# Attention runs of a four-layer hybrid stack: accumulator begun behind the first products, other order of transfers, root first on ScalarE, one table for exp and ln

## The chip, the cores and the metric

One core of a Trainium2 chip runs the whole program. The metric is the device time of one execution in microseconds; the median of three runs is the time of the kernel.

## What is computed

The reference is a stack of four layers on `x` of shape (2, 512, 256), fp32. Each layer takes a layer norm of `x`, and adds the output of a sequence part and of a feed-forward part, both computed from the normed `xn`:

```python
xn = _layernorm(x)
x = x + attention0(xn) + mixture0(xn)      # 16 heads of 128, rotary, 32 experts
xn = _layernorm(x)
x = x + state_space(xn) + spline_mlp(xn)
xn = _layernorm(x)
x = x + linear_recurrence(xn) + table_mlp(xn)
xn = _layernorm(x)
x = x + attention3(xn) + mixture3(xn)      # 16 heads of 128, biases on q, k, v and out, 8 experts
```

Attention is causal. In layer 3 the output has a bias row, `out = attn @ w_o + b_o`. The linear recurrence of layer 2 needs, once, a few numbers per state that come from exp, ln, sin, cos and a root of its 32 parameters (`mag`, `theta`, `gamma`).

## The kernel before

The batch has two sequences of 512 positions. A sequence is held as four tiles of 128 rows (`x_of`), its norm turned into `xnT` (256 features on two times 128 partitions by 512 positions), and split into a high and a low part for products of nearly full precision: `exact_product` (line 201) issues three matmuls, high by high, and the two cross terms. `acc` is an accumulator of two PSUM banks that gathers what is added to `x`: the attention heads, then the experts.

The kernel is written engine by engine, with semaphores. A `Stage` holds one function per engine, and `run(m, *stages)` (line 162) makes one block: on each engine the stages' functions run in the order in which the stages are given. A block ends on all engines before the next begins. So what sets the order of work here is the order written in each engine's function, and the order of the stages in a `run`.

There are four attention runs: layer 0 for sequence 0 (from the program's start), layer 0 for sequence 1 (from 393 us), layer 3 for sequence 0 (from 1227 us) and layer 3 for sequence 1 (from 1525 us). In each, SyncE (SP) first issues the transfers of the weights of heads 0 and 1 (`load`, `load_values`, in `first_sync`), then small tables: in layer 0 the two rotary tables, in layer 3 the biases of q, k and v, a row of ones, and the output bias `bo` twice, side by side, into `bo_row`. All the small ones count on one semaphore, `rope_loaded`. ScalarE (ACT) copies each weight's high part, GpSimd (POOL) subtracts it for the low part (`head_low`, line 812). TensorE (PE) then begins `acc`: in layer 0 by `clear_acc` (line 2190, two bf16 matmuls of zeros), in layer 3 by two fp32 matmuls of the row of ones and `bo_row` (line 1003), 512 columns each. It goes on with head 0's q and k (`project`, 12 matmuls of 512 columns), half of the values (`project_v`, 12 matmuls of 256 columns), waits until this half has been stored (`v_ready`, and in layer 3 also `v_low`), projects the other half, and comes to the scores of head 0. From there `step` runs head by head.

The vector engine (DVE) in its function of the attention first does `ahead.begin_vector` (line 1115; in the runs in which the mixture follows in the same block, that is all but the first): a memset of `logits`, a wait for the router's transfers, and in layer 3 two small multiplies that scale `router` (line 1572). Only then come the rotation or the low parts of q, k and v, and the softmax of each head.

The first run has more stages in its block:

```python
run(m, constants, first, Norm(m, 0, 0, (0, 1)).stage(), decay, heads)
```

`first` holds the copies of the first weights, `Norm(...).stage()` the layer norm (DVE takes statistics, ACT the square root in `root`, line 586, DVE the reciprocal and `xn`, PE transposes, ACT stores, DVE the low parts), and `decay` the numbers of the recurrence: `scalar` on ACT (lines 246 to 260) and `vector` on DVE (lines 267 to 291) hand results to each other. On ACT the order is that of the stages: five weight copies, then the root, then the four stores of `xnT`, then decay, then the attention. A function whose table is not the active one is preceded by a load of its table, ACT_TABLE_LOAD. Beside the first run, POOL also builds the rows of the spline weights (`SplineRows.make`, lines 373 and 379), with the low parts of the heads' weights at fixed points in between.

## Time and profile before

| what | value |
|---|---|
| median of three runs | 1826.14 us (1825.59 to 1828.66) |
| the profiled execution, its own time | 1823.52 us |
| its span | 1821.7 us |
| granted TensorE clock, mean | 0.955 |
| PE busy | 1576.4 us (87%) |
| DVE busy | 1235.7 us (68%) |
| ACT busy | 936.3 us (51%) |
| POOL busy | 691.5 us (38%) |

The times are medians over whole executions; the profile is one execution, with each instruction's start and duration on the engine that ran it. The busy shares are averages over stages with different limits. A timeline row may merge several like instructions: then its second number is the length of the stretch, and "x4" says how many there were. A number in brackets is how long the engine had been idle before, and the name behind the arrow is what released it. For a matmul, the distance between two starts is what it occupies the engine; its own duration contains the drain of the pipeline.

### The profile page before, as it was taken

The page shows a single profiled execution, that of the slowest core. Times are in us where ns is not written, and L with a number is a line of the kernel's source. Part 1 is how long each engine was busy: PE and PEld are TensorE (multiplying, and loading weights), DVE is VectorE, ACT ScalarE, POOL GpSimd, SP SyncE. Part 2 cuts the span into 40 slices and gives each one's busy share as a digit, 9 for nine tenths or more (in the row PEclk, how much of TensorE's full clock was granted, in tenths as well). Part 3 has the DMA queues.
Part 4 walks back from the last instruction along what each step waited for, and adds up shares of the span by engine and source line. Part 5 has one row for each costly group of instructions (what it writes and reads, how often), then busy time and mean ns, then how long its engine had stood idle before and what let it go on. Part 6 is the DMA issues. An engine that isn't in the chain of part 4 may idle for free. (4 is left out here: it accounts for less than half of the span.)

```text
span 1821.7 us, 26108 instructions
## 1 busy us (share of the span) xinstructions
PE 1576.4 (87%) x8448; PEld 1221.7 (67%) x8448; DVE 1235.7 (68%) x2586; ACT 936.3 (51%) x1976; POOL 691.5 (38%) x624
## 2 busy tenths in 40 slices
PE   5989868979998988867876887888999897999889
PEld 3767658967776888334533444666888685788777
DVE  5888747757777778599968996444666534666643
ACT  5555445756665565554435543224665443666543
POOL 4999833324222222075714765102221232222232
PEclk9999989989999999989998999998999898999999
DMA  3212122111112220100010000001112111111111
GB/s 111 82 64 66 35 95 81 59 51 33 46 46 86 75 76 14 49 1 1 1 49 1 0 1 6 7 10 51 41 46 75 35 69 56 33 46 46 54 68 46
DMA packets 29708, 82.47 MB, mean 45 GB/s; under 512 B 6054, under 2 KB 10924, under 8 KB 27324
## 3 DMA queue, kind: packets, MB, share of 16 engines
q1 hardware_dynamic: 28444, 75.10, 12.6%
q0 software_dynamic: 1184, 6.37, 1.0%
q8 instruction: 42, 0.69, 0.2%
q14 instruction: 38, 0.31, 0.1%
HBM read 80.41 MB, written 1.05 MB: 45 GB/s over the span
## 5 line engine op out<-in xcount | busy, mean ns | idle before, releaser
L812 POOL TENSOR_TENSOR head_low<-head,head_high 128x512 fp32r<-128x512 f32 x64 | 81.8, 1279 | 474.3 <-ACT head_high L802 473.6
L2168 POOL TENSOR_TENSOR rings<-xp,Bs 128x512 f32<-128x512 f32 x128 | 193.7, 1515 | 163.1 <-DVE state L2107 82.9
L1708 POOL TENSOR_TENSOR experts_low<-experts,experts_high 128x1536 fp32r<-128x1536 f32 (+1 forms) x64 | 144.4, 2260 | 280.6 <-ACT experts_high L1654 161.1
L1161 ACT ACTIVATE probs<-banks,neg_max 128x512 f32<-128x512 f32 (+3 forms) x256 | 131.7, 527 | 150.2 <-DVE neg_max L1072 150.2
L1956 PE MATMUL banks<-rings,ident 128*128 128x512 f32 x256 | 140.3, 648 | 66.1 <-DVE rings L2136 66.1
L2107 DVE TENSOR_TENSOR_SCAN state<-banks,rings 128x512 f32<-128x512 f32 x128 | 155.4, 1215 | 0.0
L2042 ACT ACTIVATE banks<-delta,A 128x512 f32<-128x512 f32 x128 | 88.4, 692 | 119.2 <-DVE state L2107 108.3
L201 PE MATMUL banks<-experts_high,xnT_high 128*128 128x384 f32 (+1 forms) x384 | 139.9, 364 | 8.0 <-POOL experts_low L1708 8.0
L1405 DVE SCALAR_TENSOR_TENSOR hidden<-banks,weight,act_out 128x96 f32<-128x96 f32 (+1 forms) x192 | 62.7, 368 | 115.7 <-ACT act_out L1373 115.2
L201 PE MATMUL banks<-experts_low,xnT_high 128*128 128x384 f32 (+1 forms) x384 | 137.9, 359 | 0.0
L201 PE MATMUL banks<-experts_high,xnT_low 128*128 128x384 f32 (+1 forms) x384 | 137.6, 358 | 0.0
L1373 ACT ACTIVATE act_out<-banks 128x256 f32<-128x256 f32 (+2 forms) x112 | 47.5, 424 | 172.9 <-PE banks L201 172.7
L1956 PEld LDWEIGHTS banks<-rings,ident 128*128 128x128 f32 x256 | 47.0, 199 | 114.1 <-DVE rings L2136 85.7
L915 PE MATMUL banks<-ident,probs 128*128 128x128 f32 x640 | 87.7, 287 | 40.9 <-DVE probs L1080 40.9
L1169 ACT ACTIVATE probsT<-banks 128x384 f32<-128x384 f32 (+3 forms) x192 | 88.1, 527 | 66.0 <-PE banks L915 65.2
L1070 DVE TENSOR_REDUCE row_max<-banks 128x1 f32<-128x512 f32 (+3 forms) x256 | 110.6, 483 | 10.2 <-PE banks L906 9.9
L201 PE MATMUL banks<-xnT_high,head_high 128*128 128x512 f32 x256 | 109.8, 429 | 6.3 <-POOL head_low L812 6.3
L915 PEld LDWEIGHTS banks<-ident,probs 128*128 128x128 f32 x640 | 73.1, 146 | 50.4 <-DVE probs L1080 50.3
L1043 DVE TENSOR_TENSOR rot<-banks,rope_sin 32x512 f32<-32x512 f32 x128 | 87.2, 681 | 28.3 <-PE banks L201 25.0
L201 PE MATMUL banks<-xnT_low,head_high 128*128 128x512 f32 x256 | 103.8, 405 | 0.0
L1080 DVE TENSOR_SCALAR probs<-probs,row_inv 128x512 f32<-128x512 f32 (+3 forms) x256 | 102.0, 461 | 2.3
L201 PE MATMUL banks<-xnT_high,head_low 128*128 128x512 f32 x256 | 102.8, 402 | 0.0
(284 smaller groups left out, 4752.3 us busy)
## 6 DMA issues: line engine op xcount, KB each, us to landing
head<-in_heads SPq DMA_DIRECT2D x64, 384.0 KB, 3.1
experts<-in_experts SPq DMA_DIRECT2D x16, 1152.0 KB, 5.2
experts<-in_experts SPq DMA_DIRECT2D x16, 768.0 KB, 4.3
values<-in_values SPq DMA_DIRECT2D x32, 256.0 KB, 3.2
coef<-in_spline_coef POOLq DMA_DIRECT2D x8, 768.0 KB, 4.7
idx<-in_lut_idx SPq DMA_DIRECT2D x16, 134.0 KB, 2.1
Cs<-in_w_in SPq DMA_DIRECT2D x2, 1024.0 KB, 4.9
x<-in_x SPq DMA_DIRECT2D x2, 512.0 KB, 4.5
```

What stands on the lines that cost most here:

```text
L201: last = nc.tensor.matmul(out, left[a], right[b], start=start and n == 0, stop=stop and n == 2, **kw)
L915: last = nc.tensor.transpose(out[:, (i - k) * P:(i - k + 1) * P], prob_tile(i)[:, k * P:(k + 1) * P], m.ident[:])
L1043: chain.link(nc.vector.tensor_tensor(rot[to:to + 32, which], qk_psum[of:of + 32, which], rope_sin[of:of + 32], ALU.mult))
L1070: chain.link(nc.vector.reduce_max(row_max[:, i:i + 1], score_tile(i), AXIS.X))
L1080: last = nc.vector.tensor_scalar(prob_tile(i), prob_tile(i), row_inv[:, i:i + 1], None, ALU.mult)
L1161: last = nc.scalar.activation(prob_tile(i), score_tile(i), ACT.Exp, bias=neg_max[:, i:i + 1], scale=QK_SCALE, accum_out=row_sum[:, i:i + 1])
L1169: nc.scalar.activation(probsT[:, at:at + cols], m.banks[:, k, 0:cols], ACT.Copy)\
L1708: nc.gpsimd.tensor_tensor(parts[gpar][1][:, columns], raw[gpar][:, columns], parts[gpar][0][:, columns].bitcast(FP32), ALU.subtract)\
L1956: nc.tensor.matmul(y_psum(c), m.ident[:], product[:, step % PRODUCTS], start=n == 0, stop=n == NS - 1)\
L2042: nc.scalar.activation(decay_psum(step), delta[:, c], ACT.Exp, scale=A[:, c, n:n + 1])\
L2107: nc.vector.tensor_tensor_scan(state[:, step % 3], decay_psum(step), inflow[:, step % INFLOWS], 0.0, ALU.mult, ALU.add).then_inc(scanned.s ...
L2168: nc.gpsimd.tensor_tensor(inflow[:, step % INFLOWS], du[:, c], Bs[:, n], ALU.mult)\
```

## The change

It has six parts.

1. In all four attention runs, PE begins `acc` not before `project(0, 0)` but after `project_v(0, 0)`, ahead of the wait for `v_ready`.
2. In layer 3, `bo_row` is one row of 256 instead of two; the matmul reads it twice by a stride of zero, and one transfer is gone.
3. In layer 3, the transfer of the q, k and v biases is issued second, right behind head 0's weights, and has a semaphore of its own, `bias_loaded`, for which ACT and DVE wait. PE waits for `rope_loaded` at 32 (ones and `bo`) ahead of the bias matmuls.
4. DVE does `ahead.begin_vector` after head 0's low parts (layer 3) or rotation (layer 0) and the values' low parts, right ahead of the loop over the heads.
5. In the first run, the five weight copies on ACT are no longer a stage of their own ahead of the norm's; they run inside it between the root and the stores.
6. In `decay`, ACT first loads one table set that has both exp and ln.

```diff
         act.wait_ge(loaded.sem, loaded.at(16 * len(constants)))
 
         chain = Chain(act, act_chain)
+        nc.scalar.preload_act_table_set("natural_log_exp_and_others")
         chain.all(nc.scalar.activation(lru[:, 0:1], lru_in[:, 0:1], ACT.Abs))
...
-    def stage(self):
+    def stage(self, beside_root):
...
         def scalar(act):
             self.root(act)
+            beside_root(act)
             self.store(act, 0)
             self.store(act, 1)
...
-    rope_loaded = m.sig("rope_loaded")
+    rope_loaded, bias_loaded = m.sig("rope_loaded"), m.sig("bias_loaded")
...
-        bo_row, one_row = sb("bo_row", [1, 2, D]), sb("one_row", [1, P])
+        bo_row, one_row = sb("bo_row", [1, D]), sb("one_row", [1, P])
...
     def first_sync(sp):
-        for i in range(2):
-            load(sp, i, i)
-            load_values(sp, i, i)
+        load(sp, 0, 0)
+        if not rotary:
+            sp.dma_start(biases[:], m.dram["biases3"]).then_inc(bias_loaded.sem, 16)
+        load_values(sp, 0, 0)
+        load(sp, 1, 1)
+        load_values(sp, 1, 1)
         if rotary:
             sp.dma_start(rope_cos[:], m.dram["rope_cos"]).then_inc(rope_loaded.sem, 16)
             sp.dma_start(rope_sin[:], m.dram["rope_sin"]).then_inc(rope_loaded.sem, 16)
         else:
-            sp.dma_start(biases[:], m.dram["biases3"]).then_inc(rope_loaded.sem, 16)
             sp.dma_start(one_row[:], m.dram["ones"]).then_inc(rope_loaded.sem, 16)
-            for half in range(2):
-                sp.dma_start(bo_row[:, half, :], m.dram["bo"]).then_inc(rope_loaded.sem, 16)
+            sp.dma_start(bo_row[:], m.dram["bo"]).then_inc(rope_loaded.sem, 16)
...
+        project(0, 0)
+        pe.wait_ge(values_split.sem, values_split.at(1))
+        project_v(0, 0)
+
         if rotary:
             clear_acc(m, pe)
         else:
-            pe.wait_ge(rope_loaded.sem, rope_loaded.at(64))
+            pe.wait_ge(rope_loaded.sem, rope_loaded.at(32))
             for h in range(2):
-                nc.tensor.matmul(m.acc[:, h, :], one_row[:], bo_row[:].rearrange("o a d -> o (a d)"), start=True,
-                                 stop=False, skip_group_check=True)
-        project(0, 0)
-        pe.wait_ge(values_split.sem, values_split.at(1))
-        project_v(0, 0)
+                nc.tensor.matmul(m.acc[:, h, :], one_row[:], bo_row[:].unsqueeze(1).broadcast_to([1, 2, D]),
+                                 start=True, stop=False, skip_group_check=True)
...
-        if ahead:
-            ahead.begin_vector(dve)
-        dve.wait_ge(rope_loaded.sem, rope_loaded.at(32 if rotary else 64))
         if rotary:
+            dve.wait_ge(rope_loaded.sem, rope_loaded.at(32))
             chain = Chain(dve, dve_chain)
             turn(0, 0, chain)
             turn_rest(0, chain)
         else:
+            dve.wait_ge(bias_loaded.sem, bias_loaded.at(16))
             low_of_qk(0, 0)
             low_of_qk(0, 1).then_inc(qk_ready.sem, 1)
         spread_v(0, 0, 0)
         spread_v(1, 1, 0)
+        if ahead:
+            ahead.begin_vector(dve)
...
-                run(m, constants, first, Norm(m, 0, 0, (0, 1)).stage(), decay, heads)
+                split_weights, first.scalar = first.scalar, None
+                run(m, constants, first, Norm(m, 0, 0, (0, 1)).stage(split_weights), decay, heads)
```

How the instructions stand on ACT at the program's start (`rs` is the root, `head_high` and `values_high` are the weight copies, `xnT` and `xnT_high` the stores). Before:

```order
L802 ACT_TABLE_LOAD
L802 ACTIVATE head_high_3<-head_3 128x512
L807 ACTIVATE values_high_3<-values_3 128x512
L845 ACTIVATE head_high_3<-head_3 128x256
L802 ACTIVATE head_high_3<-head_3 128x512
L807 ACTIVATE values_high_3<-values_3 128x512
L586 ACT_TABLE_LOAD
L586 ACTIVATE rs<-rs 128x4
L620 ACTIVATE xnT<-banks 128x512
L622 ACTIVATE xnT_high<-banks 128x512
L620 ACTIVATE xnT<-banks 128x512
L622 ACTIVATE xnT_high<-banks 128x512
```

After the change:

```order
L587 ACT_TABLE_LOAD
L587 ACTIVATE rs<-rs 128x4
L805 ACTIVATE head_high_3<-head_3 128x512
L810 ACTIVATE values_high_3<-values_3 128x512
L849 ACTIVATE head_high_3<-head_3 128x256
L805 ACTIVATE head_high_3<-head_3 128x512
L810 ACTIVATE values_high_3<-values_3 128x512
L621 ACTIVATE xnT<-banks 128x512
L623 ACTIVATE xnT_high<-banks 128x512
L621 ACTIVATE xnT<-banks 128x512
L623 ACTIVATE xnT_high<-banks 128x512
```

The root and the load of its table went to the front, and the separate table load of the copies is gone.

On ACT right behind, in decay (`lru`). Before:

```order
L247 ACT_TABLE_LOAD
L247 ACTIVATE lru<-lru 64x1
L248 ACTIVATE lru<-lru_in 64x1
L249 ACT_TABLE_LOAD
L249 ACTIVATE lru<-lru 64x1
L252 ACTIVATE lru<-lru 64x1
L253 ACT_TABLE_LOAD
L253 ACTIVATE lru<-lru 64x1
L254 ACTIVATE lru<-lru 64x1
L257 ACT_TABLE_LOAD
L257 ACTIVATE lru<-lru 64x1
L258 ACTIVATE lru<-lru 64x1
```

After the change:

```order
L246 ACT_TABLE_LOAD
L247 ACTIVATE lru<-lru_in 64x1
L248 ACTIVATE lru<-lru 64x1
L249 ACTIVATE lru<-lru_in 64x1
L250 ACTIVATE lru<-lru 64x1
L253 ACTIVATE lru<-lru 64x1
L254 ACTIVATE lru<-lru 64x1
L255 ACTIVATE lru<-lru 64x1
L258 ACT_TABLE_LOAD
L258 ACTIVATE lru<-lru 64x1
L259 ACTIVATE lru<-lru 64x1
L261 ACT_TABLE_LOAD
```

Before, these rows have four table loads, and a fifth (L260) follows ahead of the last root; after, they have three, of which the first stands ahead of all of decay.

On PE at the start of the third attention run, before:

```order
L163 UNCONDITIONAL_BRANCH
L170 UNCONDITIONAL_BRANCH
L1003 MATMUL acc<-bo_row,one_row 128x512 x2
L201 MATMUL banks<-xnT_high,head_high_12 128x512
L201 MATMUL banks<-xnT_low,head_high_12 128x512
L201 MATMUL banks<-xnT_high,head_low_12 128x512
```

After the change, at the same place, and then around the end of the first half of the values:

```order
L163 UNCONDITIONAL_BRANCH
L170 UNCONDITIONAL_BRANCH
L201 MATMUL banks<-xnT_high,head_high_12 128x512
L201 MATMUL banks<-xnT_low,head_high_12 128x512
L201 MATMUL banks<-xnT_high,head_low_12 128x512
```

```order
L201 MATMUL banks<-values_high_12,xnT_high 128x256
L201 MATMUL banks<-values_low_12,xnT_high 128x256
L201 MATMUL banks<-values_high_12,xnT_low 128x256
L1011 MATMUL acc<-bo_row,one_row 128x512 x2
L201 MATMUL banks<-values_high_12,xnT_high 128x256
L201 MATMUL banks<-values_low_12,xnT_high 128x256
L201 MATMUL banks<-values_high_12,xnT_low 128x256
```

The two matmuls of `bo_row` went from the front to behind the 24 first products; the fourth run shows the same, and the first two the same with the clearing of `acc`.

On DVE at the start of the third attention run, before and after the change:

```order
L176 UNCONDITIONAL_BRANCH
L1567 MEMSET logits 128x4x6
L1572 TENSOR_SCALAR router<-router,router_scale 128x8 x2
L1028 SCALAR_TENSOR_TENSOR qkT_low<-banks,biases,qkT 128x512 x2
L1062 TENSOR_TENSOR v_low_12<-banks,v_12 128x512 x2
L1126 UNCONDITIONAL_BRANCH
L1126 ISA
L1070 TENSOR_REDUCE row_max<-banks 128x1
```

```order
L176 UNCONDITIONAL_BRANCH
L1033 SCALAR_TENSOR_TENSOR qkT_low<-banks,biases,qkT 128x512 x2
L1067 TENSOR_TENSOR v_low_12<-banks,v_12 128x512 x2
L1573 MEMSET logits 128x4x6
L1578 TENSOR_SCALAR router<-router,router_scale 128x8 x2
L1132 UNCONDITIONAL_BRANCH
L1132 ISA
L1075 TENSOR_REDUCE row_max<-banks 128x1
```

The memset and the two multiplies of the router now stand between the low parts of the values and the loop of the heads, which begins with `row_max` of head 0's scores.

## Rows read from the trace of the kernel before

**Rows 1.** the chain that ended last, start of the fourth attention run: start us, us, what

```profile
1528.23 3.64 DMA bo_row<-in_bo
1531.91 3.78 PE acc L1003 x4
```

**Rows 2.** timeline, ScalarE (ACT), first attention run: start us, us, engine line, what, [idle before <- releaser]

```profile
13.06 0.63 ACT L807 ACTIVATE values_high<-values 128x512 fp32r<-128x512 f32 x1 [0.79 <-DMA values<-in_values]
13.71 1.28 ACT L586 ACT_TABLE_LOAD   x1
...
18.30 0.60 ACT L620 ACTIVATE xnT<-banks 128x512 f32<-128x512 f32 x1 [3.09 <-PE banks L613]
...
19.75 0.62 ACT L622 ACTIVATE xnT_high<-banks 128x512 fp32r<-128x512 f32 x1
...
28.90 1.02 ACT L1144 ACTIVATE qkT<-banks 64x1024 f32<-64x1024 f32 x1
```

**Rows 3.** timeline, VectorE (DVE), first attention run

```profile
6.62 0.17 DVE L570 TENSOR_SCALAR rs<-mv 128x4 f32<-128x4 f32 x1
...
22.21 0.15 DVE L270 TENSOR_SCALAR turns<-lru 64x1 int32<-64x1 f32 x1 [1.07 <-ACT lru L248]
...
23.51 0.24 DVE L534 TENSOR_TENSOR lru<-lru 64x1 f32<-64x1 f32 x1
...
24.60 1.52 DVE L534 TENSOR_TENSOR lru<-lru 64x1 f32<-64x1 f32 x1
...
27.95 2.82 DVE L1043 TENSOR_TENSOR rot<-banks,rope_sin 32x512 f32<-32x512 f32 x4
```

**Rows 4.** timeline, TensorE (PE), first attention run

```profile
21.24 1.00 PE L2190 MATMUL acc<-mask_bf,ident_bf 1*128 1x512 bf16 x2 [2.12 <-DVE xnT_low L629]
...
33.33 1.12 PE L902 MATMUL banks<-qkT 128*128 128x512 f32 x2 [1.03 <-DVE qkT L1054]
```

**Rows 5.** timeline, GpSimd (POOL), first attention run

```profile
21.32 1.39 POOL L373 TENSOR_SCALAR spline_rows<-coef,points 128x256 f32<-128x256 f32 x3 [4.11 <-DMA coef<-in_spline_coef]
...
43.48 1.27 POOL L812 TENSOR_TENSOR head_low<-head,head_high 128x512 fp32r<-128x512 f32 x1 [12.70 <-ACT head_high L802]
```

**Rows 6.** waits of POOL, 47 to 205 us: in total us, times, longest us

```profile
POOL head_low L818 <- ACT head_high L1185: 8.0, 7, 1.2
```

**Rows 7.** timeline, PE, second attention run

```profile
400.25 0.80 PE L201 MATMUL banks<-xnT_high,head_high 128*128 128x512 f32 x1 [6.30 <-POOL head_low L812]
...
407.94 0.38 PE L201 MATMUL banks<-values_high,xnT_high 128*128 128x256 f32 x1 [0.69 <-ACT v L1155]
```

**Rows 8.** timeline, PE, third attention run

```profile
1233.71 3.77 PE L1003 MATMUL acc<-bo_row,one_row 1*128 1x512 f32 x4 [8.07 <-DMA bo_row<-in_bo]
1237.42 0.79 PE L201 MATMUL banks<-xnT_high,head_high 128*128 128x512 f32 x1
...
1245.50 0.35 PE L201 MATMUL banks<-values_high,xnT_high 128*128 128x256 f32 x1 [1.50 <-DVE v_low L1062]
```

**Rows 9.** timeline, PE, fourth attention run

```profile
1535.62 0.80 PE L201 MATMUL banks<-xnT_high,head_high 128*128 128x512 f32 x1
...
1543.11 0.36 PE L201 MATMUL banks<-values_high,xnT_high 128*128 128x256 f32 x1 [1.50 <-DVE v_low L1062]
```

**Rows 10.** timeline, POOL, third attention run

```profile
1230.98 1.27 POOL L812 TENSOR_TENSOR head_low<-head,head_high 128x512 fp32r<-128x512 f32 x1 [46.53 <-ACT head_high L802]
```

**Rows 11.** timeline, POOL, fourth attention run

```profile
1529.36 1.26 POOL L812 TENSOR_TENSOR head_low<-head,head_high 128x512 fp32r<-128x512 f32 x1 [20.98 <-ACT head_high L802]
```

**Rows 12.** timeline, DVE, third attention run

```profile
1234.21 2.42 DVE L1572 TENSOR_SCALAR router<-router,router_scale 128x8 f32<-128x8 f32 x2 [6.81 <-DMA per_expert<-in_per_expert]
...
1247.82 0.69 DVE L1062 TENSOR_TENSOR v_low<-banks,v 128x512 fp32r<-128x512 f32 x1 [2.47 <-ACT v L1155]
1248.43 1.70 DVE L1070 TENSOR_REDUCE row_max<-banks 128x1 f32<-128x512 f32 x4
```

**Rows 13.** windows: stretch, us, busy of PE PEld DVE ACT POOL (instructions), PEclk, DMA, GB/s

```profile
1237.00:1242.00 5.00, 5.00 (x12) 3.62 (x12) 0.75 (x1) 0.69 (x1) 0.00 (x0) 0.50 0.11 42
```

More of the change, by code:

```diff
@@ L1203, in scalar @@
         if not rotary:
-            act.wait_ge(rope_loaded.sem, rope_loaded.at(64))
+            act.wait_ge(bias_loaded.sem, bias_loaded.at(16))
         spread_rest(0)
@@ L1248, in close @@
             s.close(PAIRS)
+        rope_loaded.close(32)
         if rotary:
             qk_rest_ready.close(HEADS)
-            rope_loaded.close(32)
         else:
-            rope_loaded.close(64)
+            bias_loaded.close(16)
             qk_high.close(2 * HEADS)
```

## The prediction

> **What bounds the kernel now.** The page says that PE is busy for 87% of the span, but the change touches only the first microseconds of the four attention runs, so the shares say little; what counts is the last wait in each of these stretches. I read the chain that ended last first, then the timeline of each engine at each start, then POOL's waits.
>
> The chain shows the start of the fourth run: the transfer of `bo_row` (3.64 us), then the matmuls that put it into the accumulator (3.78 us) [rows 1]. PE has the first products behind them. In the third run it is the same: PE is idle for 8.07 us until `bo_row` lands, and the first product starts at 1237.42 [rows 8], although its weights were ready when POOL's `head_low` ended, at 1230.98 + 1.27 = 1232.25 [rows 10]. In the second run nothing is ahead of the products but `head_low` [rows 7].
>
> In the first run the root comes late: DVE had its input at 6.79, while ACT, with the copies ahead of it, was done with the last copy at 13.69 and only then loaded the root's table [rows 2, 3]. The stores of `xnT` (18.30 to 20.37) wait for PE, thus for the root. Then ACT and DVE play decay back and forth: DVE's part starts at 22.21, it is free for the rotation at 27.95, ACT for `qkT` at 28.90 [rows 2, 3], and the first scores start at 33.33, released by DVE [rows 4]. The reader should see that both queues are in order: heads wait behind decay.
>
> **First run: root first, one table.** The root can run at 6.8, beside nothing. DVE's `xn` and PE's transposes come some 8.5 us earlier, long before ACT is done with the copies, which their transfers hold at 13.06 + 0.63 = 13.69 as before. So the first store starts at 13.7 instead of 18.30: 4.6 us. That holds if the root were a table load (1.28) later, too. The four stores take 20.37 - 18.30 = 2.07, end at 15.76; DVE's last low part ends 4.6 earlier, and the clearing of the accumulator (21.24, about 0.9 us up to the first product) has left that place, so PE starts its products near 16.6.
>
> Decay on ACT: one load of 1.28 in front, then Abs and two Exp without a load between: to 17.8, where DVE's part starts, 22.21 - 17.8 = 4.4 earlier. From there to the rotation it took 27.95 - 22.21 = 5.74 us. In that is one operation of 1.52 which takes 0.24 a microsecond before [rows 3], while POOL was at work on the spline rows from 21.32 [rows 5]. POOL's start hangs on a transfer issued behind copies that do not move. DVE's chain will be over before 21.32, so I take these 1.28 off, and 0.3 for the second load and small gaps on ACT: 5.74 - 1.6 = 4.1, rotation at 21.9. That is 6.0 us earlier. Bounds: 4.7 with the stretched operation still there, 6.2. ACT then has sine and root with two loads, ready for `qkT` about 22.9 (28.90 before), and PE's products, 7.0 us for both kinds from a standstill in the second run (400.25 to 407.94, less 0.69) [rows 7], end near 23.7: neither comes last. **-6.0 us.**
>
> The page "ScalarE: Activation LUTs" of the Trainium skill (section "What ACT_TABLE_LOAD costs") gives for each switch, besides the 1283 ns of the load, about 1380 ns of drain. Three loads are gone, so by it the sum would be up to 4.1 us better (an estimate from that page). Here the load follows the copy by 0.02 us and lasts 1.28 [rows 2], which is all that I count.
>
> **Second run.** The clearing was done in idle time before the products; now it lies in the 0.69 us in which PE waits for `v` [rows 7]. Two matmuls took about 0.9 us up to the next product at the slow clock [rows 4], half at full clock: covered, 0 (at most +0.4). If that wait went, they would cost 0.4. The memset of `logits` is now ahead of `row_max`, which waits for the scores anyway: 0.
>
> **Third and fourth runs, PE.** The first product starts 0.05 behind `head_low`, as in the second run: 1232.30 instead of 1237.42, and, from 1529.36 + 1.26 = 1530.62 [rows 11], 1530.67 instead of 1535.62 [rows 9]: 5.12 and 4.95 earlier. The biases' transfer is now ahead of the values and pushes them by one issue of some 0.5 us, but the low parts of the values are needed only after 5 us of products. The clock takes part back. The 12 products of q and k ran at a granted clock of 0.50 [rows 13], the 1.2 GHz level, and both kinds of products took 1245.50 - 1.50 - 1237.42 = 6.58 and 1543.11 - 1.50 - 1535.62 = 5.99, with the bias matmuls in front. From a standstill it was 7.00 in the second run. I take 7.00: +0.42 and +1.01.
>
> Then the bias matmuls. At the slow clock they took 1237.42 - 1233.71 = 3.71. Behind the products the clock should be up, so 1.86. They lie in PE's wait for `v_low`, 1.50 [rows 8, 9]: +0.3 stands out in each (bounds 0 and, at the slow clock, +2.2). `bo_row` landed at 1233.71 and is needed near 1239.3: its transfer is hidden now, and would show again if it came over 5 us later. Reading 256 elements twice instead of 512: the same columns, 0.
>
> **Third and fourth runs, DVE.** The memset and two multiplies move from idle time to between `v_low` and `row_max`. There DVE has no gap: `v_low` 1247.82 + 0.69, `row_max` at 1248.43 [rows 12]. They took 2.42 us for the two multiplies, but with POOL at work on the weights. The nearest quiet row is the 0.17 of a like operation on 128x4 [rows 3]; POOL is idle at the new place. Three of 0.17 are **+0.5** each run (bounds 0 and 2.5). Left in front they would have cost as much: the multiplies ended at 1236.6, and the first low part is now wanted near there.
>
> Sum: third run -5.12 + 0.42 + 0.3 + 0.5 = -3.9, fourth -4.95 + 1.01 + 0.3 + 0.5 = -3.1, first -6.0, second 0: **-13.0 us**. Against the profiled execution, 1823.52, that is 1810.5; it stands 2.62 below the median, so for the median I predict 1826.14 - 13.0 = **1813.1 us**.
>
> **Rivals.**
> *POOL paces the first run.* It starts the spline rows at 21.32 whatever ACT does. If its work set the pace of the heads, the 6.0 would be gone: 1819.1. Against it: POOL is idle 12.70 us until head 2's copy at 43.48 [rows 5], and later waits for ACT 1.2 us in every second head, 7 times [rows 6]. It follows.
> *The clock stays down.* If PE, idle until its first product, is still at the slow level after the products, the values' products take about 0.6 more and the bias matmuls 1.86 more in each of the last runs: 4.9 in all, 1818.0. For it: 0.50 through the q and k products of the third run even with matmuls in front [rows 13]. Against it: in the second run both kinds took 7.00, less than 12 x 0.427 + 12 x 0.213 = 7.7 (0.427 is 512 columns at 1.2 GHz).
> *Slower.* The shift of the first run changes how POOL's spline work meets DVE's operations. If each of 16 heads had one more operation stretched by 1.28 [rows 3], that is +20.5: 1833.6. It decides from 0.8 us per head on. Against it: POOL restarts on ACT's copy for head 2, so it keeps its place relative to the heads. The Trainium skill ("GPSIMD Engine Reference", Specifications) says that POOL shares its SBUF interfaces with DVE, for some of DVE's operations; the stretch from 0.24 to 1.52 agrees.
> *A table switch costs twice its row.* Then three loads fewer give another 3 x 1.28 = 3.8: 1809.3. The gap of 0.02 us speaks against it. The drain named above, of the Trainium skill's page "ScalarE: Activation LUTs", would act like this.
> *The change does nothing that lasts*: what the starts gain is lost later to a wait that I don't see, as on transfers: 1826.1.
>
> **How the numbers follow.** Forecast 0.75, clock 0.11, POOL 0.06, twice the row 0.03, nothing 0.03, slower 0.02. A difference of 0.2% (3.7 us) is about what a measurement tells from none. The first four are faster by more: 0.95, same 0.03, slower 0.02. The range starts from 1813.1: with the bounds for products as before (-1.4), bias matmuls covered (-0.6) and free multiplies (-1.0) it is 1810.1, and half the spread of the runs shown (1.5) gives 1808.6, taken as 1808.5; upwards the clock and the POOL case, with the second run's 0.4, give 1819.5.
>
> **What would show it.** In the profile after: the root near 6.8, the first store near 13.7, DVE's rotation near 22 and the first scores near 27.3 (before 33.33), head 2's `head_low` on POOL near 37.5; in the last two runs PE released by `head_low`, bias matmuls of some 1.9 us behind the values, `v_low` to `row_max` with 0.5 between. It is wrong if POOL no longer waits for ACT, if the bias matmuls take 3.7 there, or if the runs end no earlier than their starts moved.

## The result, and the profile after

The changed kernel took 1812.87 us, median of five runs (1807.48 to 1820.19), beside 1826.14 (1821.61 to 1828.66) for the kernel before on the same chip: a ratio of 0.9931, 95% interval 0.9914 to 0.9948, which is 13.3 us by the medians. The prediction was 1813.1, in a range of 1808.5 to 1819.5. (Here and below a ratio and its interval come from all executions of both kernels, so a ratio can differ from the quotient of the two medians by up to 0.001.)

The profile after shows a span of 1818.4 us, only 3.3 less than before. It belongs to the slowest of the five runs (1820.19), so its ends must not be read as the gain; its starts can be, after subtracting what lies before them.

The busy times are nearly those of before: PE 1584.0 us, DVE 1232.2, ACT 932.5, POOL 691.9.

Timeline of ACT, first attention run, answering to [rows 2]:

```profile
6.94 0.20 ACT L587 ACTIVATE rs<-rs 128x4 f32<-128x4 f32 x1 [4.90 <-DVE rs L571]
...
13.31 0.63 ACT L810 ACTIVATE values_high<-values 128x512 fp32r<-128x512 f32 x1 [1.07 <-DMA values<-in_values]
13.85 0.58 ACT L621 ACTIVATE xnT<-banks 128x512 f32<-128x512 f32 x1
...
15.91 1.28 ACT L246 ACT_TABLE_LOAD   x1
17.20 0.20 ACT L247 ACTIVATE lru<-lru_in 64x1 f32<-64x1 f32 x1
...
17.67 0.20 ACT L249 ACTIVATE lru<-lru_in 64x1 f32<-64x1 f32 x1
...
20.83 0.20 ACT L258 ACTIVATE lru<-lru 64x1 f32<-64x1 f32 x1 [0.77 <-DVE lru L286]
...
22.65 1.02 ACT L1150 ACTIVATE qkT<-banks 64x1024 f32<-64x1024 f32 x1
```

DVE in the same stretch, answering to [rows 3]. The operation that took 1.52 before is the one at 19.92:

```profile
17.91 0.15 DVE L271 TENSOR_SCALAR turns<-lru 64x1 int32<-64x1 f32 x1 [1.24 <-ACT lru L249]
...
19.92 0.15 DVE L535 TENSOR_TENSOR lru<-lru 64x1 f32<-64x1 f32 x1
...
21.72 2.82 DVE L1048 TENSOR_TENSOR rot<-banks,rope_sin 32x512 f32<-32x512 f32 x4
...
30.61 0.17 DVE L1077 TENSOR_SCALAR neg_max<-row_max 128x4 f32<-128x4 f32 x1
```

PE there, with the clearing in its new place, answering to [rows 4]:

```profile
23.37 0.60 PE L2196 MATMUL acc<-mask_bf,ident_bf 1*128 1x512 bf16 x2
24.35 0.39 PE L201 MATMUL banks<-values_high,xnT_high 128*128 128x256 f32 x1 [0.37 <-ACT v L1161]
...
27.11 1.12 PE L906 MATMUL banks<-qkT 128*128 128x512 f32 x2 [1.06 <-DVE qkT L1059]
```

POOL there, answering to [rows 5], and below it POOL's waits from 40 to 200 us, answering to [rows 6] (in total us, times, longest us):

```profile
21.15 1.39 POOL L374 TENSOR_SCALAR spline_rows<-coef,points 128x256 f32<-128x256 f32 x3 [4.01 <-DMA coef<-in_spline_coef]
...
37.26 1.27 POOL L815 TENSOR_TENSOR head_low<-head,head_high 128x512 fp32r<-128x512 f32 x1 [6.67 <-ACT head_high L805]
```

```profile
POOL head_low L821 <- ACT head_high L1191: 8.0, 7, 1.2
```

A whole queue has moved: the scores start at 27.11 instead of 33.33, 6.22 earlier, and POOL comes 6.22 earlier too (43.48 to 37.26) and still waits for ACT, seven times, as before. It follows. The last weight copy on ACT started at 13.31 instead of 13.06, held by its transfer; with these 0.25 us taken out, the queue moved by 6.5.

The third run, PE, answering to [rows 8]:

```profile
1231.08 0.80 PE L201 MATMUL banks<-xnT_high,head_high 128*128 128x512 f32 x1 [6.75 <-POOL head_low L815]
...
1236.37 0.41 PE L201 MATMUL banks<-values_high,xnT_high 128*128 128x256 f32 x1
...
1238.06 1.98 PE L1011 MATMUL acc<-bo_row,one_row 1*128 1x512 f32 x4
1239.97 0.39 PE L201 MATMUL banks<-values_high,xnT_high 128*128 128x256 f32 x1
```

and DVE behind it, answering to [rows 12]:

```profile
1243.36 0.69 DVE L1067 TENSOR_TENSOR v_low<-banks,v 128x512 fp32r<-128x512 f32 x1 [3.87 <-ACT v L1161]
1244.00 0.20 DVE L1578 TENSOR_SCALAR router<-router,router_scale 128x8 f32<-128x8 f32 x1
1244.00 0.08 DVE L1573 MEMSET logits<- 128x24 f32 x1
1244.11 0.22 DVE L1578 TENSOR_SCALAR router<-router,router_scale 128x8 f32<-128x8 f32 x1
1244.24 1.15 DVE L1075 TENSOR_REDUCE row_max<-banks 128x1 f32<-128x512 f32 x2
```

The chain of the fourth run, answering to [rows 1]: the bias row is gone from its head, the products are led by head 0's own transfer.

```profile
1522.50 3.45 DMA head<-in_heads
...
1525.97 0.64 ACT head_high L805
...
1526.67 1.27 POOL head_low L815
...
1527.99 7.09 PE banks L201 x24
1535.08 1.91 PE acc L1011 x4
```

Where did the rest of the profile's gain go? Windows of the second mixture (branch 1's, between the last attention head and the join), same instructions, of the kernel before and of the changed one (columns: length, busy us of PE, PEld, DVE, ACT, POOL, then the granted clock of PE, where 1.00 is 2.4 GHz and 0.50 is 1.2 GHz, its two levels; then the share and rate of the transfers):

```profile
584.97:732.68 147.71, 127.46 (x828) 121.08 (x827) 112.96 (x338) 85.20 (x161) 41.76 (x16) 0.97 0.16 54
```

```profile
580.22:730.92 150.70, 130.42 (x828) 124.09 (x827) 113.02 (x338) 85.33 (x161) 41.75 (x16) 0.94 0.15 53
```

DVE, ACT and POOL have the same busy time within 0.13 us, PE 2.96 more, the stretch is 2.99 longer: it is the clock, 0.94 instead of 0.97, in code that the change does not touch. Two more stretches read the same: the first mixture (from 237.00 to 392.89 before, from 230.77 to 388.63 now) is 1.97 longer at 0.94 instead of 0.96, and the first recurrence (from 1124.69 to 1175.15, and from 1122.86 to 1175.95) 2.63 longer at 0.87 instead of 0.93.

### The profile page after: what moved, and what is told of

Read it like the earlier page. It is cut to its first block and busy times, and to the rows that moved or that the text cites. A ratio compares the mean times of both kernels' runs of the same rounds, so it can differ in the third digit from the quotient of the medians.

```text
span 1818.4 us, 26103 instructions
## 1 busy us (share of the span) xinstructions
PE 1584.0 (87%) x8448; PEld 1231.3 (68%) x8448; DVE 1232.2 (68%) x2586; ACT 932.5 (51%) x1973; POOL 691.9 (38%) x624
```

## The experiments

Two kinds of reading: times against the kernel before on the same chip (nothing under some 2 us can be told there), and marks in each profile. The marks are the start of the first `neg_max` of a run, or the last operation of a mixture or recurrence, minus the same mark in the profile before, so that a minus is time gained; in brackets what was added since the mark above, where it is large. Mixtures 0 and 1 are those of layer 0, mixture 2 that of the third attention run, and the end is that of the fourth.

```
                    after        same again    first run only  rest only     row kept
run 1, head 0       -6.2         -6.5          -7.4            -0.2          -6.8
run 1, head 14      -6.2         -6.8          -7.8            -0.5          -6.9
mixture 0 ends      -4.3 (+2.0)  -6.6          -8.9 (-1.1)     -1.0 (-0.5)   -5.0 (+1.9)
run 2, head 0       -4.7         -6.7          -9.2            -1.2          -7.6 (-2.7)
mixture 1 ends      -1.8 (+3.0)  -6.6          -9.5            -1.1          -7.0
layer 1 ends        -1.8         -6.6          -9.6            -1.2          -6.1 (+0.9)
recurrence 0 ends   +0.8 (+2.6)  -6.5          -9.6            -1.2          -3.4 (+2.7)
recurrence 1 ends   -1.3 (-2.1)  -6.6          -6.9 (+2.8)     -1.3          -3.6
run 3, head 0       -4.0 (-2.7)  -8.9 (-2.3)   -6.4            -6.5 (-5.2)   -8.9 (-5.2)
mixture 2 ends      -2.8 (+1.2)  -9.4 (-0.5)   -6.1            -7.3 (-0.9)   -9.0
run 4, head 0       -4.6 (-1.8)  -13.2 (-3.8)  -6.4            -11.1 (-3.8)  -13.2 (-4.2)
end                 -3.3         -13.3         -6.4            -11.4         -13.1
```

**The changed kernel again.**

> The changed kernel once more, with a new profile. Theory A (what the starts gained is kept; the rest of the first profile's loss, 8 us between the sum of the four starts and the end, is the granted clock, which differs from one execution to the next): first scores of the first run again at 27.1, the time 1810 to 1815 in the median, and the ends of the mixtures stand elsewhere against the kernel before than in the first profile (-4.3, -1.8, -2.8, -3.3 there), by 1 us or more in at least one. Theory B (the change itself costs 3 us in the first mixture and 3 in the second): the same losses again, -4 and -2 within 0.5. In both: if the fall of the clock behind the bias matmuls (theory C) is a rule, the products right behind them start 0.21 us apart in the third and the fourth run again; if it was chance (theory D), 0.12 apart in at least one.

1810.11 us (1808.47 to 1815.13) beside 1826.06: 0.9911, interval 0.9895 to 0.9927. In this profile the same mixture took 147.87 at 0.97 and no mark between run 1 and run 3 moved by over 0.3. The 8 us missing in the first profile came with that execution, not with the change: theory A. The clock's fall behind the bias matmuls came again in run 3 and not in run 4, so it is no rule (theory D). The median lies 16.0 below the kernel before, 3 more than forecast, though the four starts of this profile add up to 12.7 (6.5, 0.1, 2.3, 3.8) and its span is 13.3 less. The profile of before is of an execution 2.6 below its own median, which is the size of that gap; nothing in the four starts accounts for it. Such jumps of 2 to 3 us, of both signs, stand also in kernels that share nothing but the untouched code (the table).

**The first run's part alone.** Against the kernel before:

```diff
+        nc.scalar.preload_act_table_set("natural_log_exp_and_others")
...
-    def stage(self):
+    def stage(self, beside_root):
...
             self.root(act)
+            beside_root(act)
...
-                run(m, constants, first, Norm(m, 0, 0, (0, 1)).stage(), decay, heads)
+                split_weights, first.scalar = first.scalar, None
+                run(m, constants, first, Norm(m, 0, 0, (0, 1)).stage(split_weights), decay, heads)
```

> The kernel before with the two parts in the first run alone (root first, one table). Theory A: -6.2 us, 1820; the first max of head 0 at 30.6 instead of 36.84, and as much earlier in every head up to 14. Rival (POOL paces the heads, or the gain is eaten up by the end of the run): within 2 us of the kernel before.

1818.77 us (1814.61 to 1820.58): 0.9954, 0.9939 to 0.9969. Of the 7.4 at head 0, 0.9 come from transfers: the last copy on ACT started at 12.15 instead of 13.06. The rest is 6.5, as in the changed kernel with its own 0.25 taken out, and it is kept through all heads: theory A.

**The rest alone.** Against the changed kernel it is this diff backwards, nothing else.

> The changed kernel with the first run's ACT order and tables as before, so the parts on the accumulator, the transfers and the router alone. The clearing in the first run is behind the products, but the run's start hangs on ACT and DVE: 0 there. Theory A with C: second run -0.4, third -2.7, fourth -1.8, together -5 us, 1821. By the prediction's terms, with a clock that stays up: -7.0, 1819.

1817.10 us (1812.10 to 1820.83): 0.9951, 0.9936 to 0.9967. That is more than either expectation (5 and 7 us). In the profile runs 3 and 4 gained 5.2 and 3.8, and the clock stayed up behind the bias matmuls in both, against theory C. Both halves gain alone: the medians put 7.3 us on the first run's part and 9.0 on the rest, 16.3 together, beside 13.3 and 16.0 in the two measurements of the whole.

**Ones and bias row loaded once, and kept.** Against the changed kernel:

```diff
-            sp.dma_start(one_row[:], m.dram["ones"]).then_inc(rope_loaded.sem, 16)
-            sp.dma_start(bo_row[:], m.dram["bo"]).then_inc(rope_loaded.sem, 16)
+            if norm_here:
+                sp.dma_start(m.one_row[:], m.dram["ones"]).then_inc(m.sig("row_loaded").sem, 16)
+                sp.dma_start(m.bo_row[:], m.dram["bo"]).then_inc(m.sig("row_loaded").sem, 16)
...
+        if not rotary:
+            pe.wait_ge(m.sig("row_loaded").sem, 32)
+            for h in range(2):
+                nc.tensor.matmul(m.acc[:, h, :], m.one_row[:], m.bo_row[:].unsqueeze(1).broadcast_to([1, 2, D]),
...
         project(0, 0)
...
-            for h in range(2):
-                nc.tensor.matmul(m.acc[:, h, :], one_row[:], bo_row[:].unsqueeze(1).broadcast_to([1, 2, D]),
```

> The changed kernel with the row of ones and the output bias loaded once, in the first run, and the bias matmuls in front in the third and fourth run, in the idle time before head_low (8 us, they need 3.7 at the slow clock). Theory C (the one-row matmuls behind the products make the clock fall, 1.5 us of slow products in each run, and stick out by 0.3): the next products start 0.12 apart, and each of the two runs is 1.8 us shorter up to the first max of head 0: 3.6 us less than the changed kernel, 1809. Theory D (chance): 0.3 each, 0.6 in all, 1812. Rival E: matmuls in front leave the PE idle again until head_low, no gain for the clock of the first 12 products.

1810.83 us (1805.02 to 1814.09): 0.9909, 0.9891 to 0.9927, not to be told from the changed kernel, and between theory C's 1809 and theory D's 1812. In the profile its runs 3 and 4 gain most in this table (-5.2 and -4.2): from the start of the last of the values' first products to the start of their second ones it takes 1.78 instead of 2.12, and the products behind run at full clock.

**The root alone.** The kernel before, with the first part's diff less its first line; decay keeps its five table loads:

```diff
             self.root(act)
+            beside_root(act)
```

> The kernel before, with only the norm's root moved ahead of the copies on ScalarE; decay keeps its five table loads. Theory A (the root's place gives its part by itself, ACT's decay behind it moves as one block): first store near 13.3 to 13.7, sine near 22.3 (27.08 before), rotation on DVE near 23.2, first neg_max of head 0 4.6 to 5.0 earlier than 36.84, about 32.0; time 1821.3. Rival B (table loads are what counts, the root's place gives little since ACT's chain of loads sets the end): under 3 us at head 0, time 1823.5 or more. Rival C (the root's place gives all of the 6.2 us): head 0 at 30.6, time 1819.9.

1820.42 us (1818.38 to 1826.47, 12 runs) beside 1825.90: 0.9976, 0.9962 to 0.9989. ACT there:

```profile
13.62 0.63 ACT L808 ACTIVATE values_high<-values 128x512 fp32r<-128x512 f32 x1 [0.54 <-DMA values<-in_values]
14.15 0.58 ACT L620 ACTIVATE xnT<-banks 128x512 f32<-128x512 f32 x1
...
22.92 0.20 ACT L257 ACTIVATE lru<-lru 64x1 f32<-64x1 f32 x1
```

The store comes 4.15 earlier than before, the sine 4.16, `neg_max` of head 0 3.96. The last copy came 0.56 later than before, by its transfer; without that it is 4.5. Theory A, a little under its number. DVE, whose operations up to there are all short (0.15 us), waits 2.31 us for ACT's sine: ACT's table loads now pace the exchange. From mark to mark to the end nothing moves by more than 0.7, and the end is 5.0 earlier.

**The one table alone.** Against the kernel before:

```diff
+        nc.scalar.preload_act_table_set("natural_log_exp_and_others")
```

> The kernel before, with only the one table for exp and ln loaded ahead of decay; the root stays behind the copies. Theory A (the two loads saved lie beside DVE's part, which here still holds the operation of 1.52 us because POOL starts at 21.3, so sine waits for DVE instead): ACT's Exp that starts DVE's part ends at about 22.2 as before, the sine is only 0.6 us earlier (26.5), head 0's neg_max 0.6 earlier, time 1825.5. With A the parts do not add up: 4.8 + 0.6 are less than the 6.2 of both together, because the long operation on DVE goes only when both are done. Rival B (two loads of 1.28 lie on the path): head 0 2.6 earlier, time 1823.5.

1825.34 us (1821.63 to 1831.37, 12 runs): 1.0002, 0.9987 to 1.0016. No gain, and in the profile head 0 was 3.5 us *later*. DVE there:

```profile
22.32 0.15 DVE L271 TENSOR_SCALAR turns<-lru 64x1 int32<-64x1 f32 x1 [1.24 <-ACT lru L249]
...
22.98 0.42 DVE L278 SCALAR_TENSOR_TENSOR lru<-lru 64x1 f32<-64x1 f32 x1
...
24.07 1.71 DVE L535 TENSOR_TENSOR lru<-lru 64x1 f32<-64x1 f32 x1
...
27.86 1.18 DVE L290 TENSOR_TENSOR lru<-lru 64x1 f32<-64x1 f32 x1 [0.36 <-ACT lru L259]
...
29.43 2.82 DVE L1044 TENSOR_TENSOR rot<-banks,rope_sin 32x512 f32<-32x512 f32 x4
```

and POOL beside it:

```profile
23.94 1.83 POOL L380 TENSOR_TENSOR spline_rows<-spline_rows,term 128x768 f32<-128x768 f32 x1
...
27.22 1.81 POOL L380 TENSOR_TENSOR spline_rows<-spline_rows,term 128x768 f32<-128x768 f32 x1
```

Each long operation of DVE begins while a POOL instruction runs and ends with it: 24.07 + 1.71 = 25.78 beside 23.94 + 1.83 = 25.77, and 27.86 + 1.18 = 29.04 beside 27.22 + 1.81 = 29.03. The 1.52 of before ends at 26.12, POOL's instruction (24.29, 1.82 us) at 26.11. So in these rows an operation that is held lasts for what is left of POOL's instruction when it begins. Not every one is held: all of them with one tile as their only input took 0.15 us.

ACT saves its two loads and then waits 3.06 us for DVE ahead of the sine (27.53, before 27.08). DVE's part, from `turns` to the rotation, took 7.11 instead of 5.74 [rows 3]. The last copy had even come 0.97 us earlier (12.09), but one of DVE's small operations on `rs` (L209, 1.10 us, ending with POOL's `values_low`) ate that before the first store. The rotation is 1.48 later than before; the other 2.0 of the 3.5 are the clock. PE was idle for 3.34 us ahead of the values' second products, and some 0.7 us after it had gone on the granted clock fell (1.00 from 28 to 31, 0.50 from 33.5 to 37), so that head 0's scores ran slowly:

```profile
34.81 2.08 PE L903 MATMUL banks<-qkT 128*128 128x512 f32 x2 [1.12 <-DVE qkT L1055]
```

against 1.12 [rows 4]. Theory A had the mechanism, and too little of it: I took the long operation of before as a constant.

**The same, with POOL's spline rows held back** until DVE is done with decay:

```diff
         load(1)
+        pool.wait_ge(m.sig("lru_dve").sem, m.sig("lru_dve").at(3))
         pool.wait_ge(self.loaded.sem, self.loaded.at(16))
```

> As the run with the one table alone (root behind the copies), but POOL waits for DVE's last decay operation before it starts the spline rows (20.99 in that run, here near 25). Theory A (DVE's small operations get long because POOL works beside them, and this is what ate the two saved loads): all decay operations on DVE take 0.15 to 0.2 again, DVE's part starts at 22.3, sine near 25.2, rotation near 26.1 (29.43 there, 27.95 before), head 0's neg_max near 35.0, that is 1.8 earlier than before; POOL, which had 12.7 us to spare, still waits for head 2's copy; time 1824.1. Rival B (the long operations have another cause): they stay, rotation at 28 or later, head 0 no earlier than 36.5, time 1825.5 or more.

1822.36 us (1820.28 to 1825.54, 9 runs) beside 1825.87: 0.9983, 0.9973 to 0.9993. DVE, then POOL:

```profile
23.00 0.15 DVE L271 TENSOR_SCALAR turns<-lru 64x1 int32<-64x1 f32 x1 [1.24 <-ACT lru L249]
...
26.25 0.15 DVE L290 TENSOR_TENSOR lru<-lru 64x1 f32<-64x1 f32 x1 [0.36 <-ACT lru L259]
...
26.79 2.82 DVE L1045 TENSOR_TENSOR rot<-banks,rope_sin 32x512 f32<-32x512 f32 x4
```

```profile
26.86 1.39 POOL L375 TENSOR_SCALAR spline_rows<-coef,points 128x256 f32<-128x256 f32 x3 [8.71 <-DVE lru L292]
...
42.32 1.26 POOL L814 TENSOR_TENSOR head_low<-head,head_high 128x512 fp32r<-128x512 f32 x1 [6.06 <-ACT head_high L804]
```

No operation of decay on DVE is over 0.15 us, and its part takes 3.79. POOL, 5.9 us later, still waits 6.06 for ACT. Taking POOL's work away from beside DVE is the only edit between these two kernels, so it is shown that POOL's work there made DVE's operations long. (The line numbers of these rows are those of their own kernels.) The rotation is 1.16 earlier than before although ACT's last copy was 0.65 later; that is the 1.8 of theory A, whose time of 1824.1 the interval takes in (1820.9 to 1824.6).

**No bias.** Against the changed kernel:

```diff
-        if rotary:
-            clear_acc(m, pe)
-        else:
+        if not rotary:
             pe.wait_ge(rope_loaded.sem, rope_loaded.at(32))
-            for h in range(2):
-                nc.tensor.matmul(m.acc[:, h, :], one_row[:], bo_row[:].unsqueeze(1).broadcast_to([1, 2, D]),
-                                 start=True, stop=False, skip_group_check=True)
+        clear_acc(m, pe)
```

> The changed kernel, with the accumulator of the last two attention runs cleared instead of filled with the output bias: this leaves the output bias of the projection out. Against the changed kernel run again (1810.1). Theory C (it is the slow one-row matmuls of the bias, 1.9 us of them, behind which the granted clock falls): values' second products at full clock in both runs (1.3 to 1.5 us for the 15 matmuls, not 2.1 to 2.3), and their start follows the first products' end by 1.77, not 2.12: 0.35 saved in each run plus the clock's part, time 1808 to 1809.4. Rival D (it is the wait for v_low itself, with or without bias matmuls): the slow stretch of 2.1 to 2.3 shows in at least one of the two runs, the time 1809.4 to 1810.1. If both runs are clean, C gains but is not proved, since three of six were clean with the bias there.

This kernel leaves the output bias out. 1809.47 us (1805.41 to 1815.65): 0.9916, 0.9895 to 0.9938. From the start of the last of the values' first products to that of their second ones it takes 1.78 in both runs, and both ran on at full clock. Runs 3 and 4 gained 5.7 and 4.3. By time it can't be told from the changed kernel, and two clean starts prove nothing yet, since three of six were clean with the bias there.

**The accumulator in front again**, all else as changed:

```diff
-        project(0, 0)
-        pe.wait_ge(values_split.sem, values_split.at(1))
-        project_v(0, 0)
         if rotary:
             clear_acc(m, pe)
...
+        project(0, 0)
+        pe.wait_ge(values_split.sem, values_split.at(1))
+        project_v(0, 0)
```

> The changed kernel, with the accumulator begun ahead of the first products again, in all four runs; root, table, order of transfers and the place of the router's three operations stay as changed. Theory A (what the last two runs gain is only that PE no longer waits for bo_row ahead of its products): PE idle until bo_row lands, at 0.5 us earlier than before because one transfer of it is gone and one issue fewer is ahead of it, then 3.7 us of bias matmuls; the first products of runs three and four 4.3 later than in the changed kernel; time 1810.1 + 2 x 3.8 = 1817.7, about that of the first run's part alone (1818.8). In the first run the clearing comes ahead of the products, in idle time: nothing. Rival B (the order of transfers brings the gain, the place of the accumulator little): time under 1814.

1819.87 us (1815.98 to 1821.79, 9 runs): 0.9963, 0.9949 to 0.9978. Runs 3 and 4 gain 0.5 and 0.1 there, not the 1.8 to 5.2 of the three profiles with the bias matmuls behind. Theory A's 1817.7 lies in the interval (1816.6 to 1821.9), rival B's 1814 does not. The clearing in front cost the first run nothing (head 0 at -6.1, with the last copy 0.45 late). So what the last two runs gain is the accumulator's place; the other transfers are worth half a microsecond at most.

**The bias matmuls twice:**

```diff
-            for h in range(2):
+            for h in (0, 1, 0, 1):
```

> The changed kernel, with the two bias matmuls issued twice in each of the last two runs (the second pair begins the accumulator anew, the values are the same). Theory C (granted clock falls behind these matmuls, the more of them the surer): the 15 matmuls behind them run at the slow clock in both runs (2.1 to 2.3 us instead of 1.3 to 1.4), and the second pair, uncovered, costs 1.9 where the clock holds and up to 3.7 where it falls: 1810.1 + 2 x 1.9 + about 2 = 1816. Rival E (only a late rise of the clock decides, that is first products of 6.8 us or more): slow only where the first products took that long; time 1814. If the second pair were hidden too (the wait for v_low is longer than it looks): 1810.

1815.40 us (1814.60 to 1817.90, 5 runs) beside 1825.87: 0.9942, 0.9928 to 0.9955. The gap is 3.84 instead of 2.12: 1.72 each, uncovered. Windows of its third run, columns as above: products of q and k, bias matmuls, what follows, and the head's scores:

```profile
1228.70:1233.00 4.30, 4.27 (x11) 3.39 (x12) 0.45 (x1) 2.08 (x4) 4.30 (x4) 0.54 0.36 91
...
1235.00:1238.50 3.50, 3.50 (x9) 1.28 (x9) 0.78 (x2) 0.57 (x1) 0.00 (x0) 1.00 0.02 5
1238.50:1239.50 1.00, 1.00 (x9) 1.00 (x9) 0.00 (x0) 0.00 (x0) 0.00 (x0) 1.00 0.00 0
1239.50:1243.00 3.50, 3.50 (x15) 2.57 (x13) 1.57 (x5) 1.88 (x2) 0.00 (x0) 0.51 0.00 0
```

The clock stays up through 3.7 us of bias matmuls, falls to 0.51 a microsecond behind them, with PE never idle, and is back at 1243. The same happened in run 4. Since it fell only after most of the values' second products, these took 1.67 and 1.50 us (start of the first to start of the last), not the 2.1 to 2.3 of theory C, and the scores paid instead: to `neg_max` they took 4.33 and 4.50 instead of 3.43. Rival E is out, because the first products had taken only 5.9 and 6.1 us.

**Row kept, and the router's three operations in front.** The diff of the kept row, and:

```diff
+        if ahead:
+            ahead.begin_vector(dve)
         if rotary:
             dve.wait_ge(rope_loaded.sem, rope_loaded.at(32))
...
         spread_v(1, 1, 0)
-        if ahead:
-            ahead.begin_vector(dve)
```

> A version meant to beat both: the changed kernel with the ones and the bias row loaded once and kept (the bias matmuls in front of the products in the last two runs, where PE waits anyway), and the router's memset and two multiplies in front of DVE's work again. Theory A (the place of these three operations behind v_low costs 0.26 us of DVE time per run, in front they cost nothing because the first values' low part is needed 5 us later): scores to neg_max 3.17 again instead of 3.43, first products start as in the changed kernel, the fifteen matmuls behind v_low at full clock in both runs, 1.77 between first and second values' products: 0.34 + 0.26 less in each run, 1810.8 (the row-kept run) - 0.5 = 1810.3, not to be told from the changed kernel by its time. Rival B (in front they delay the values' low part and so the products): values' first products start later than 5.3 behind the first product, time 1811 or more.

1809.51 us (1805.19 to 1811.37, 5 runs): 0.9903, 0.9889 to 0.9917. DVE of its third run:

```profile
1231.87 2.54 DVE L1578 TENSOR_SCALAR router<-router,router_scale 128x8 f32<-128x8 f32 x2 [7.66 <-DMA per_expert<-in_per_expert]
1234.32 1.40 DVE L1033 SCALAR_TENSOR_TENSOR qkT_low<-banks,biases,qkT 128x512 fp32r<-128x512 f32 x2
...
1239.86 1.70 DVE L1075 TENSOR_REDUCE row_max<-banks 128x1 f32<-128x512 f32 x4
```

In front the two multiplies are long (2.54) and cost nothing; `row_max` starts 0.61 behind `v_low` (1239.25), and scores to `neg_max` is 3.17 again. It has the lowest median of all versions that compute the whole result, but it can't be called faster than the changed kernel: it leads the second measurement by 0.6 us and the first by 3.4, and these two measurements of one kernel differ by 2.8.

## Why the prediction was right, step by step

**First run: -6.0 predicted, -6.2 in the profile, -6.5 with the late copy taken out.** The last figure is 6.4 to 6.5 in all eight profiles of kernels that have both parts. Step by step: root 6.8 (6.94), first store 13.7 (13.85), products 16.6 (16.72 by the timeline), DVE's part 17.8 (17.91), rotation 21.9 (21.72), `qkT` 22.9 (22.65), scores 27.3 (27.11), head 2's low copy 37.5 (37.26). (`xn` came 8.1 us earlier, not 8.5; nothing waited for it.) The step that could have failed was the stretched operation, of which I only said that DVE's chain would be over before POOL starts at 21.3. That is what happened: all but its last three operations have ended by 20.80. The experiments show how much hung on it. Alone, the root gives 4.0 to 4.5 and the table nothing; together 6.2 to 6.5. The table's two loads count only where DVE's part is out of POOL's way, moved there by the root or, as when POOL was held back, by keeping POOL away. So the sum was right as a sum, and would have been wrong as a list of parts.

**The table switch.** The load of 1.28 stands at 15.91, directly behind the last store (15.28 + 0.61 = 15.89), and the activation at 17.20, 0.01 behind the load's end. So a switch is worth its row, and the rival at twice the row fell. The Trainium skill ("ScalarE: Activation LUTs", "What ACT_TABLE_LOAD costs") adds a drain of about 1380 ns to each switch; no such time shows on ACT here, and the measurement decides.

**Second run: 0.** The clearing lies in the wait for `v`: 0.37 us of it are left in the first run [after, PE at 24.35]. Covered. The step at run 2 was -0.5 and -0.1 in the two profiles of the changed kernel; the -2.7 with the row kept, in a kernel that is the same there, has 1.8 from head 0's transfer (3.21 us from issue to landing instead of 5.02) and 0.9 from behind it, where the clock rose earlier and the first products took 5.46 instead of 6.72.

**Last two runs: -3.9 and -3.1.** PE's first product 1231.08, less 1.30 that was there already: 5.04 earlier than 1237.42 (predicted 5.12); in the fourth 1527.99, less 2.78, 4.85 earlier than 1535.62 (4.95). The exposed part of the bias matmuls is 2.12 - 1.78 = 0.34 (0.3). Three terms were off in size:
- Router: 0.26, not 0.5. The memset (0.08) also started at 1244.00, beside the first multiply, and the multiplies took 0.20 and 0.22 but follow each other by 0.11. And "left in front they would have cost as much" was wrong: there they cost nothing.
- Products at 7.00, that is 6.72 up to the start of the last of them. Measured by that mark: 6.78 and 6.81 in the first profile, then 7.01 and 6.09, and with the rest alone 5.46 and 5.99. The eight kernels with matmuls in front have 5.7 to 6.5, with a mean of 6.09; the four with them behind (bias twice among these) 5.46 to 7.01, with 6.27. So +0.42 and +1.01 fit the first profile (+0.48 and +1.10), but by luck: on the average the kernels differ by 0.2 a run, which is less than the scatter, and the rest is when the clock happens to rise.
- The clock *behind* the bias matmuls, which I had only as a rival with another cause. That rival's own sign, bias matmuls of 3.7 us, did not come: they took 1.9 in all six starts. The fall behind them cost 1.2 us in three of six: 0.9 in the values' second products and 0.3 in the scores in the first profile (3.71 to `neg_max`, 3.43 where it was clean), 0.7 and 0.5 in the second.

Over both runs the first two made the forecast some 0.5 and 1.0 too slow, the third some 1.2 too fast on the average. That they nearly cancel is luck; the mechanism, PE no longer waiting for `bo_row` ahead of its products, is what the prediction had right. Clean starts gain 5.2 and 3.8 (rest alone), disturbed ones 2.7 and 1.8 (the first profile), and the predicted 3.9 and 3.1 lie between.

**Rivals.** POOL paces: no, it waits for ACT as before. Nothing lasts: no, the shift at head 0 is there at head 14 and, but for the clock's jumps, at the end. Slower, through POOL's spline work meeting DVE: the mechanism exists and was shown, but in another place. It stretched decay when only the table was changed; in the changed kernel POOL keeps its place to the heads. The Trainium skill ("GPSIMD Engine Reference", Specifications) says that POOL shares its SBUF interfaces with DVE for some of DVE's operations, those with two SBUF inputs among them; the trace agrees: operations of DVE with two such inputs became up to 1.7 us long, while the rotation, which reads a PSUM bank, took 0.70 us an operation beside POOL (2.82 for four) and with POOL idle in head 1 (1.39 for two, at 31.41). The router's multiplies, with one tile and one scalar per partition as inputs, were held as well: 1.19 and 1.31 us beside POOL before, 0.20 and 0.22 with POOL idle.

## What to carry to other kernels

When two engines hand work back and forth beside a third one, ask for each shortened step which of their operations then falls beside the third: two edits that are worth 4 and 0 alone were worth 6 together, and holding back the third engine, which had time to spare, made the 0 worth something too. A wait in front of a queue is best spent on work that is ready; if its input is late, move the work into a later wait or bring its input for good. Judge by several executions: in one profile of this kernel the clock hid 8 of the 11 us that its own starts had gained, and only marks, read stretch by stretch, showed it.

## What was not expected of the hardware

**The granted clock fell behind one-row matmuls although PE was never idle.** The changed kernel's third run, windows as above (bias matmuls, then the values' second products):

```profile
1238.00:1240.00 2.00, 2.00 (x7) 0.69 (x5) 0.78 (x2) 0.60 (x1) 0.00 (x0) 1.00 0.00 0
1240.00:1243.00 3.00, 3.00 (x15) 2.90 (x15) 0.00 (x0) 0.27 (x1) 0.00 (x0) 0.54 0.03 5
```

From the first to the last of these products (start to start) it then takes 2.3 us instead of 1.37. The fall came in both runs of the first profile and in the third run of the second (2.1 us). It did not come in the fourth run of the second, nor in either run with the rest alone: three of six. With twice the matmuls it came in two of two. Where these matmuls stood in front of the products it came in none of 16 starts (eight kernels), and with the bias left out in none of two. That it goes with one-row matmuls behind the products is thus shown by counts; what about them the clock's control sees, and why three starts were spared, stays open. In the six starts it came where the products had taken 6.78 us or more, that is where the clock had risen late, but with twice the matmuls also after 5.9 and 6.1. A late rise alone is not enough: in the second run of the repeated kernel the products took 6.78 us too, with the clearing behind them, and the clock stayed up.

**The clock also fell behind a wait of 3.34 us** (the table alone, first run), and **stretches of untouched code vary by 2 to 3 us** with the clock alone, in steps, in both directions: the second mixture took 150.70 us at 0.94 in one execution of the changed kernel and 147.87 at 0.97 in another. What sets them was not tried.
